# Sixteen-head attention layer: the order in which SyncE issues the weight loads of the next heads

## The reference

```python
q = split_heads(hidden_states @ wq)
k = split_heads(hidden_states @ wk)
v = split_heads(hidden_states @ wv)
q = _apply_rotary(q, cos, sin)
k = _apply_rotary(k, cos, sin)
valid = (k_pos > q_pos - WINDOW) & (k_pos <= q_pos)
attn = jnp.einsum('bhqd,bhkd->bhqk', q, k) * scale
attn = jax.nn.softmax(jnp.where(valid, attn, neg), axis=-1)
out = jnp.einsum('bhqk,bhkd->bhqd', attn, v)
return out.transpose(0, 2, 1, 3).reshape(Bsz, Ln, NUM_HEADS * HEAD_DIM) @ wo
```

## Time and profile before

| | us |
|---|---|
| median of 3 runs | 741.87 |
| lowest and highest | 740.88, 742.18 |
| the profiled execution | 742.18 |
| its span in the trace | 740.4 |
| what lies around the span | 1.78 |

### The profile page before, as it was taken

The page is one execution under the profiler, slowest core; times in us unless marked ns, Lnnn a source line. Parts: engine busy times, 40 slices in busy tenths (PEclk is TensorE's granted clock), DMA queues, the critical chain, the costliest instruction groups (busy, mean ns, idle before and its releaser), DMA issues. The chain is left out here.

```text
span 740.4 us, 13269 instructions
## 1 busy us (share of the span) xinstructions
PE 657.4 (89%) x4740; PEld 495.0 (67%) x4740; DVE 520.8 (70%) x1059; ACT 348.1 (47%) x750; POOL 320.2 (43%) x255
## 2 busy tenths in 40 slices
PE   4797999999789999999999999989967799877788
PEld 1353555568468887878798887879767547645666
DVE  3348577664679979797979986655445775669794
ACT  2266121120256575655555574644623452297732
POOL 0100488700167657474747577794384131300100
PEclk9999999999999999999999999999989899989889
DMA  9501000000420101010101001113212000100001
GB/s 302 249 1 58 2 1 1 1 1 1 152 83 13 46 9 35 14 38 18 35 21 35 21 11 60 32 33 140 75 48 58 0 1 1 35 0 1 1 0 58
DMA packets 14581, 31.34 MB, mean 42 GB/s; under 512 B 1837, under 2 KB 8587, under 8 KB 13901
## 3 DMA queue, kind: packets, MB, share of 16 engines
q1 hardware_dynamic: 12637, 26.46, 10.4%
q0 software_dynamic: 1536, 3.15, 1.5%
q10 hardware_dynamic: 368, 1.18, 0.6%
HBM read 26.59 MB, written 5.24 MB: 43 GB/s over the span
## 5 line engine op out<-in xcount | busy, mean ns | idle before, releaser
L576 PE MATMUL bank<-zone 128*128 128x256 f32 (+1 forms) x408 | 142.1, 348 | 23.7 <-POOL zone L2024 9.5
L577 PE MATMUL bank<-zone 128*128 128x256 f32 (+1 forms) x408 | 134.1, 329 | 0.0
L578 PE MATMUL bank<-zone 128*128 128x256 f32 (+1 forms) x408 | 133.9, 328 | 0.0
L2030 POOL TENSOR_TENSOR arena<-arena 128x512 f32<-128x512 f32 x64 | 82.3, 1286 | 63.5 <-ACT arena L1236 63.4
L576 PEld LDWEIGHTS bank<-zone 128*128 128x128 f32 x408 | 79.5, 195 | 44.6 <-issue 16.0
L2035 POOL TENSOR_TENSOR arena<-arena 128x512 f32<-128x512 f32 x64 | 83.2, 1301 | 26.7 <-DVE arena L1619 18.0
L578 PEld LDWEIGHTS bank<-zone 128*128 128x128 f32 x408 | 79.8, 196 | 6.3
L577 PEld LDWEIGHTS bank<-zone 128*128 128x128 f32 x408 | 79.9, 196 | 3.5
L1255 ACT ACTIVATE arena<-arena 128x256 f32<-128x256 f32 (+1 forms) x128 | 62.0, 487 | 42.2 <-DVE arena L1628 41.6
L557 PE MATMUL bank<-xT,arena 128*128 128x512 f32 x160 | 78.3, 629 | 2.1 <-ACT xT L1127 0.8
L1644 DVE SCALAR_TENSOR_TENSOR x<-bank,arena,x 128x256 f32<-128x256 f32 x128 | 53.1, 470 | 23.3 <-PE bank L578 17.6
(11 more groups left out here) (288 smaller groups left out, 1336.7 us busy)
## 6 DMA issues: line engine op xcount, KB each, us to landing
arena<-in_qk SPq DMA_DIRECT2D x16, 256.0 KB, 2.6
arena<-in_tern SPq DMA_DIRECT2D x1, 3072.0 KB, 21.7
arena<-in_wv SPq DMA_DIRECT2D x8, 256.0 KB, 2.9
arena<-in_wo SPq DMA_DIRECT2D x16, 128.0 KB, 2.1
arena<-in_wr SPq DMA_DIRECT2D x1, 1792.0 KB, 10.2
lB<-in_lB SPq DMA_DIRECT2D x1, 1288.5 KB, 24.2
arena<-in_lA SPq DMA_DIRECT2D x1, 1282.5 KB, 15.1
x<-in_x SPq DMA_DIRECT2D x1, 1024.0 KB, 12.7
```

Source lines behind the costliest of these rows:

```text
L576: pe.matmul(dst, lhi, rhi, start=(n == 0), stop=False)
L577: pe.matmul(dst, lhi, rlo, start=False, stop=False)
L578: last = pe.matmul(dst, llo, rhi, start=False, stop=(n == len(terms) - 1 and not open_end))
L2030: pool.tensor_tensor(qraw[:, j, :], qraw[:, j, :], cosT[:, at], ALU.mult).then_inc(cos_done, 1)
```

## The change

The line that loads `wr[0]` is written behind the three small functions instead of ahead of them; since these only define code, SP issues it at the same place. The loads of the heads are regrouped: for each pair first the `wv`, then for each of its two heads the `wqk` and the `wo`. The values that are waited for stay as they were; what changes is which wait stands ahead of which. The loop now runs seven times instead of six, and one `wqk` load stays behind it.

```diff
-            sp.dma_start(wr[0], dram["wr"][:, 0:EXP_A]).then_inc(wr_loaded, 16)
...
-            next_wqk(0)
-            next_wv(0)
-            next_wqk(1)
-            with sp.Fori(0, SPLIT // 2 - 1) as i:
-                next_wo(i * 2)
-                next_wqk(i * 2 + 2)
-                next_wv(i + 1)
-                next_wo(i * 2 + 1)
-                next_wqk(i * 2 + 3)
-            next_wo(SPLIT - 2)
+            sp.dma_start(wr[0], dram["wr"][:, 0:EXP_A]).then_inc(wr_loaded, 16)
+            with sp.Fori(0, SPLIT // 2) as i:
+                next_wv(i)
+                for c in range(2):
+                    next_wqk(i * 2 + c)
+                    next_wo(i * 2 + c)
             next_wqk(SPLIT)
-            next_wo(SPLIT - 1)
```

## The result

The changed kernel took 747.51 us (median of 7 executions, 744.91 to 749.74), and the kernel before, beside it on the same chip, 741.87 us (7 executions). The ratio is 1.0076, with a 95% interval of 1.0048 to 1.0104: slower by 5.6 us, where 1.5 us had been forecast, and above the forecast range. Its profiled execution, 753.78 us with a span of 751.9 us, is the highest of all of them, so I never set its whole span against the 740.4 us of before. I set distances within the trace against each other.

The account below looks back on a forecast made before the run. TensorE, busy 89% of the span, was taken to bound the kernel. All loads cost 0 except one 1.46 us stall in head 11, so 741.87+1.5 = 743.4 us, range 742.0 to 745.3.

Parts of the forecast that it names:

- the place and the mechanism: End of head 11: head 13's `wqk` load, issued behind `wo`, comes late for ACT, and TensorE waits 1.46 us.
- the covers everywhere else: Cost 0 outside head 11: cover 1.1 us in even heads, 2.5 in odd, 1.2 in head 12, 0.5 in head 13.
- the 5.3+0.7 of the sum: Head 13: the xg load lands 5.3 us after issue plus 0.7 queued, at 509.8, wanted at 512.02; cost 0.
- the term of head 11: Head 11: `wqk` lands at 464.93, so TensorE starts piece 2 at 466.2 instead of 464.74, a 1.46 us stall.
- landing 460.78+4.15: Head 11: the `wqk` load lands 4.15 us behind the `wo` issue at 460.78, that is at 464.93.
- Cost 1.46 us: Head 11: TensorE's stall ahead of piece 2; 1.05 us if the landing is unqueued, 2.95 with the longest one.
- the queueing of loads: Loads issued in a row: a queued 256 KB load lands 0.69 us behind the one ahead.
- The longest landing that I had allowed for, +5.65: `wqk` issued 1.15 us behind `wo` and landing after the trace's longest 4.5 us; in head 11 a 2.95 us stall.
- TensorE needs it 4.0 us after: TensorE starts piece 2 4.0 us after the old start of ACT's piece 0 copy, 460.73 to 464.74 in head 11.
- the clock counted as a rival: Behind head 11's pause the clock falls, costing 1 to 1.5 us; part of the rival at 744.7, chance 0.24.
- a late load in head 13: Head 13's load lands 1 us later than thought and takes 0.5 us; shares the rival's chance of 0.24.
- The first rival: Ahead of head 13 the clock stays at 2.4 GHz, giving back up to 1.3 us: 742.1 us, chance 0.22.

Follow-up runs that it names:

- the runs with more instructions: Changed kernel plus 96 or 48 long-satisfied waits on TensorE ahead of head 11: 747.67 us (ratio 1.0086) and 744.6 us (1.0042).
- again: The changed kernel timed and profiled once more without an edit: 751.48 us against 748.85 for the kernel before, ratio 1.0040.
- head 11 as before: Changed kernel, but head 13's `wqk` load is issued ahead of the wait for head 11's `wo`, last two pairs written out: 747.9 us, ratio 1.0002.
- The filled pause: Changed kernel with piece 1 of the values projected three times in head 11, so TensorE is busy where it would wait: 749.6 us, ratio 1.0015.
- 48 waits: Changed kernel with 48 long-satisfied waits (24 more instructions) on TensorE ahead of head 11: 744.6 us, ratio 1.0042.
- no sends beside: Changed kernel with all five of POOL's sends of head 11 moved to the head's start: 751.33 us against 748.79, ratio 1.0037.

## Why the prediction was wrong, point by point

**Right: the place and the mechanism.** One load of fifteen makes the loss, and it is the one named. Taking it back leaves 1.0002, making it alone gives 1.0026. What failed is the size of the stall, and what the clock adds to it.

**Right: the covers everywhere else.** Even heads, odd heads 1 to 9, and head 12 (ACT stands still for 2.71 us, TensorE for nothing new) cost nothing. Head 13 had a cover of about 0.5 us, as forecast (the copy of piece 0 ends at 514.8 us, and TensorE's next piece starts at 515.3), and the runs with more instructions showed how thin that is. The load of xg landed 5.9 us after its issue, as the 5.3+0.7 of the sum had it, and nobody waited for it.

**Wrong: the term of head 11**, "landing 460.78+4.15" and "Cost 1.46 us". Counted from the `wo` issue, with the rows of the two traces of the changed kernel:

| | forecast | after | again |
|---|---|---|---|
| ACT starts its rounding | +4.22 | +5.68 | +5.04 |
| TensorE wants the result | +3.96 | +3.24 | +3.26 |
| pause | 1.46 | 3.61 | 2.95 |

(The copy ends and TensorE starts 1.17 us behind ACT's start in both, against 1.2 in the sum.) More than half of the miss is the first line, 0.8 to 1.5 us, and it isn't the queueing of loads, which I had priced: in head 5 the same three loads gave +4.24. By the table above it goes with the packet of instructions, which heads 2 to 9 don't have, so the rows of heads 4 and 5 couldn't show it. `wqk` landed at +5.6 and +5.0 where +4.15 had been taken. In the two traces of the changed kernel the slow `wv` issue goes with the packet as well, and no run parts the two there; but where `wv` was issued fast, ACT started later still (+5.87, +5.88). The longest landing that I had allowed for, +5.65, was the right bound, for a cost of 2.95 us, but I gave it no chance of its own.

The second line is 0.7 us. "TensorE needs it 4.0 us after" was read from one trace in which the clock had been at 0.50 just ahead, at 446 to 448 us, so that TensorE was late itself. At 2.4 GHz it arrives sooner, while the `wo` issue doesn't move (15.77 us behind the head's first product before, 15.75 after). This makes the pause longer than forecast, but it isn't a loss against the trace of before, where the head had lost that time to the slow clock: there the product behind the pause comes 2.9 and 2.2 us late, less than the pauses of 3.61 and 2.95. Against a head 11 at full clock it is a loss in part. With head 11 as before, the `wo` issue of head 12 stands 36.16 us behind the first product of head 11, and 36.64 before: 0.5 us of the 0.7 to 0.9 is kept. A forecast pause that is measured against a slow clock is too short.

**Wrong: the clock counted as a rival.** The fall behind the pause was priced at "1 to 1.5 us", with a chance of 0.24 that it shared with a late load in head 13. The filled pause shows 1.5 us, so the price was right, and the fall was there in both traces of the changed kernel. Behind the pauses of 1.52 and 1.53 us (48 waits, no sends beside) the clock did hold, so it was fair to keep it a rival for a pause of 1.5 us. With a pause of 3 us it came in both traces, but 2.56 us didn't bring it, so how likely it was isn't shown. It belonged in the sum with its price times its chance. Together: delay 2.2 to 2.9, clock 1.5, and 0.2 to 0.3 that `wo` of head 12 is later in the filled trace as well (17.16 against 16.91), which makes the 4.1 and 4.6 us by which the distance grew against before.

**The first rival, and why nothing came back.** It wanted the clock to hold ahead of head 13. That happened: in 490 to 492 us and behind it the granted clock is 1.00 and not 0.50. Window from the first product behind the wait for POOL to the same product as in the earlier trace rows:

```profile
495.43:510.90 15.47, 13.99 (x112) 11.66 (x113) 8.23 (x19) 7.85 (x20) 13.75 (x13) 1.00 0.06 17
```

TensorE is busy for 13.99 us and not 15.51, and the stretch takes 15.47 us, as long as before: its faster products run into a wait of 1.47 us for DVE at 504.95. The 1.3 us of slow clock in head 13 had been covered work, not a price. So the rival's condition came true and its gain didn't. In the trace of the changed kernel again the clock did fall there (0.50 in 496 to 498 us), and SP's `wo` issues of heads 12 and 13 stand as far apart: 21.23 us, 21.17 in the first trace, 21.23 before.

**Open.** The loss was 5.6 us in the first comparison and 2.6 us in the second. The profiled traces differ by only 0.5 us in the distance, so that isn't explained by what they show; whether head 13 stalls in some of the executions without a trace wasn't seen. It is open too why only some of the issues beside an instruction packet are slow, what the packet does to a load, and what decides where it falls.

## What to carry to other kernels

A load whose issue is moved behind a wait of another engine has to be priced at the place where its cover is thinnest and against everything that shares the DMA engines there, the instruction transfers among it; here the later passes of the loops, heads 2 to 9, had none, so their landing times were too good for head 11. Read the moment at which TensorE wants a result from a stretch at full clock, since a slow stretch in the one trace lends a cover that isn't there in the next. And where a pause of TensorE is forecast, add the products that run at the low clock behind it: at 3 us of pause that was another 1.5 us where the clock fell.

## What the runs showed of the hardware that I had not expected

- With one 0.02 MB packet of the instruction queue beside it, a 128 KB load landed after 2.4 to 3.3 us and not 1.95 to 2.25 (10 loads against 157), or the third of three loads after 4.2 to 4.9 us and not 2.7, while the DMA engines were idle for most of the last 1.5 us (share 0.01). The Trainium skill (DMA: Bandwidth & Descriptors, section Anatomy of one DMA) gives about 2.0 us plus the bytes at 436 GB/s for a DMA that GpSimd issues. The loads here are issued by SyncE, and the prediction didn't say so when it used the figure. Taken over to them it is an estimate, 2.6 us for 256 KB. The median landing of 2.7 us agrees with it; the 4.9 us of one load doesn't, though the traffic beside it ran at up to 383 GB/s (464 to 465 us). The Trainium skill (DMA: Bandwidth & Descriptors, section Queues, rings and completion order) says that a load's semaphore write on a DMA engine lands only after every earlier write of that engine, across its queues. That would let one other packet hold back a load whose bytes are through, as in the trace without sends; no run here separates this from the packet just taking its turn.
- The clock fell to the 1.2 GHz level behind pauses of 3.61, 2.95 and 1.98 us, and not behind 2.56 and 1.53 us; and behind the wait for POOL ahead of head 13 in the trace of before (2.16 us), but not of after (2.13 us). Even behind the wait of 0.80 us for DVE ahead of head 11 it fell in the trace of before (0.50 at 446 to 448 us), and not in that of after (1.00). The length of a pause alone doesn't tell.
- SP's issue of a DMA took 0.68 to 1.88 us in 13 cases of 854, each beside an instruction packet; the usual issue of a weight load takes 0.33 us. The run with 48 waits has three of the 13: 0.77 us for `wqk`, 1.28 for `xg` and 1.45 for a store.
- 48 instructions that only wait, with nothing to wait for, held TensorE for 3.5 us (4.3 less the 0.8 of before), some 70 ns each.
